# A two-layer graph attention kernel: the order of aggregation, projection and transposition in steps 3 to 5 of layer 0

## The reference, cut to what matters

```python
# layer 0 (adj holds only 0 and 1, so only a0 takes part)
e     = leaky(einsum('bid,bjd->bij', x * a0, x))        # leaky slope 0.2
alpha = sigmoid(where(adj == 1, e, -max))
x1    = layernorm(x + einsum('bij,bjd->bid', alpha, x) + bias)
# layer 1
Hh = x1 @ W;  s = Hh @ a_src;  d = Hh @ a_dst
e  = where(adj != 0, exp(-leaky_relu(s[:, :, None] + d[:, None, :], 0.2)), 0)
h  = elu((e @ Hh) / rowsum(e))
out = layernorm(x1 + h)
```

## Time and profile before

| | us |
|---|---|
| median of 3 runs | 1378.3 (1376.89 to 1379.58) |
| profiled execution, its own time | 1379.31 |
| span of the profiled execution | 1377.5 |
| PE busy | 1277.8 (93%) |
| DVE busy | 1030.4 (75%) |
| ACT busy | 855.3 (62%) |
| POOL busy | 841.3 (61%) |

### The profile page before, as it was taken

How to read it: one execution, slowest core, us unless ns; L and a number is a source line. 1 busy time by engine, 2 the same in 40 slices (tenths; PEclk the granted TensorE clock), 3 DMA queues, 4 the chain that set the end, 5 groups by cost and what they waited for, 6 DMA issues and landing times.

```text
span 1377.5 us, 27394 instructions
## 1 busy us (share of the span) xinstructions
PE 1277.8 (93%) x7874; PEld 1142.0 (83%) x7874; DVE 1030.4 (75%) x2594; ACT 855.3 (62%) x2129; POOL 841.3 (61%) x1228
## 2 busy tenths in 40 slices
PE   3899999999999999999999999999999998999986
PEld 3788888888888888988888888888888888888875
DVE  3677878777787777778777787877778777787864
ACT  3665757567574765757567574765757567574642
POOL 4465838557394765838567394765838567394732
PEclk9999999999999999999999999999999999999998
DMA  6344251623406143251623406143250623406001
GB/s 142 61 77 101 40 103 47 110 72 63 109 11 126 57 82 97 42 105 40 110 72 65 107 16 121 57 86 93 45 109 32 110 72 65 107 15 122 27 5 33
DMA packets 190352, 101.73 MB, mean 74 GB/s; under 512 B 140656, under 2 KB 173808, under 8 KB 190320
## 3 DMA queue, kind: packets, MB, share of 16 engines
q1 hardware_dynamic: 171888, 67.79, 20.9%
q0 software_dynamic: 18432, 33.56, 14.5%
HBM read 84.55 MB, written 16.78 MB: 74 GB/s over the span
## 4 chain that ended last, share of the span: by engine, by line
PE 39%; POOL 24%; DVE 19%; issue 11%; ACT 5%; DMA 1%; DVEq 0%; POOLq 0%; SPq 0%; ACTq 0%
POOL coef_lo L368 13%; PE acc_bank L1207 11%; PE hh_bank L1186 5%; DVE coef L867 5%; PE acc_bank L1088 4%; PE acc_bank L1090 4%; PE acc_bank L1089 4%; PE lg_bank L1088 3%; PE lg_bank L1090 3%; PE lg_bank L1089 3%; POOL var_eps L376 3%; POOL rstd L379 2%; POOL rstd L389 2%; DVE stats L907 2%; DVE reluP L902 2%
## 5 line engine op out<-in xcount | busy, mean ns | idle before, releaser
L1207 PE MATMUL acc_bank<-H,coef 128*128 128x258 f32 x2048 | 468.9, 383 | 10.4 <-ACT reluP L607 9.1
L1207 PEld LDWEIGHTS acc_bank<-H,coef 128*128 128x128 f32 x2048 | 382.7, 190 | 72.1 <-issue 18.1
L368 POOL TENSOR_TENSOR coef_lo<-coef,coef_hi 128x1024 fp32r<-128x1024 f32 x128 | 306.0, 2392 | 77.4 <-ACT coef_hi L553 75.6
L1088 PE MATMUL acc_bank<-h_hi,coef_hi 128*128 128x256 f32 x1024 | 297.9, 291 | 1.8 <-issue 1.8
L1090 PE MATMUL acc_bank<-h_hi,coef_lo 128*128 128x256 f32 x1024 | 286.9, 280 | 0.0
L1089 PE MATMUL acc_bank<-h_lo,coef_hi 128*128 128x256 f32 x1024 | 286.8, 280 | 0.0
L867 DVE SCALAR_TENSOR_TENSOR coef<-tr_bank,E_col,codeT 128x256 f32<-128x256 f32 x512 | 209.1, 476 | 39.3 <-PE acc_bank L1207 36.8
L1088 PEld LDWEIGHTS acc_bank<-h_hi,coef_hi 128*128 128x128 f32 x1024 | 195.2, 191 | 2.9 <-issue 2.0
L1089 PEld LDWEIGHTS acc_bank<-h_lo,coef_hi 128*128 128x128 f32 x1024 | 195.8, 191 | 0.0
L1090 PEld LDWEIGHTS acc_bank<-h_hi,coef_lo 128*128 128x128 f32 x1024 | 195.5, 191 | 0.0
L553 ACT ACTIVATE coef_hi<-coef 128x1024 fp32r<-128x1024 f32 x128 | 135.6, 1060 | 86.5 <-DVE coef L806 86.1
(11 more groups left out here) (76 smaller groups left out, 2280.3 us busy)
## 6 DMA issues: line engine op xcount, KB each, us to landing
code_nat<-in_adj POOLq DMA_DIRECT2D x128, 256.0 KB, 5.0
x_raw<-in_x SPq DMA_DIRECT2D x16, 1024.0 KB, 5.6
out<-x SPq DMA_DIRECT2D x128, 128.0 KB, 1.7
codeT<-code_nat SPq DMA_TRANSPOSE x128, 3.3
W_ext<-in_L_gnn_W SPq DMA_DIRECT2D x1, 256.0 KB, 2.8
score<-in_L_gnn_a SPq DMA_DIRECT2D x1, 256.0 KB, 6.8
bias_bc<-in_L_gnn_bias SPq DMA_DIRECT2D x1, 128.0 KB, 3.5
a_col<-in_L_gnn_a SPq DMA_DIRECT2D x4, 1.0 KB, 2.1
```

The costliest lines, as they stand in the source:

```text
L368: nc.gpsimd.tensor_tensor(coef_lo[:, t % 4, :, :], blocks(coef[:, t % 4, :]), f32(coef_hi[:, t % 4, :, :]), ALU.subtract).then_inc(S.lo0, 1)
L1088: nc.tensor.matmul(dst, lhs_hi, rhs_hi, start=first, stop=False)
L1207: ins = nc.tensor.matmul(acc_bank[t % 2][:, 0:HC], coef[:, SLOT1[t], J * P:(J + 1) * P], H[:, J, :], start=J == 0, stop=J == NT - 1)
```

## The change

In PE's list, steps 3 to 6 now run the aggregation of `t` first, then `project(t-3)`, then `T(t-2)`. Step 2 loses `project(0)`, which goes to step 3; step 6 gets a second projection, `project(4)`, at its end, so that from step 7 on the order is the old one. The transpositions of columns (`spread_G`) of tiles 0 to 2 move from step 5 to step 6.

In ACT's list, `keep_H(t-3)` and `keep_x1T(t-2)` of steps 3 to 6 move from the head of the step to behind `high0` and `watch_codes`; in steps 3 to 5 `watch_codes` moves behind `high0`. In step 5 the pair now stands ahead of `norm1` of the graph before.

In DVE's list, `low_xT` stands ahead of `norm0` in steps 2 to 5, as it did before only in step 5.

```diff
 # ACT
                 for t in range(NT + 1):
-                    if t >= 3:
+                    if t >= 7:
                         keep_H(F, b, t - 3, prev, False)
-                    if t >= 2:
+                    if t == 2 or t >= 7:
                         keep_x1T(F, b, t - 2, prev)
                     if nxt and t in XT_STEP:
                         high_xT(F, b + 1, XT_STEP[t], False)
-                    if t < 6:
+                    if t < 3:
                         watch_codes(b, t)
                     if 1 <= t and t + 3 < NT:
                         high0(F, b, t + 3, prev)
+                    if 3 <= t < 6:
+                        watch_codes(b, t)
+                    if 3 <= t < 7:
+                        keep_H(F, b, t - 3, prev, False)
+                        keep_x1T(F, b, t - 2, prev)
                     if t == 5 and prev:
                         norm1(F, b - 1, NT - 1)
 # DVE
-                    if nxt and t == 5:
+                    if nxt and t in XT_STEP:
                         low_xT(F, b + 1, XT_STEP[t], False)
                     if t >= 1:
                         norm0(F, b, t - 1, prev)
-                    if nxt and t < 5 and t in XT_STEP:
-                        low_xT(F, b + 1, XT_STEP[t], False)
 # PE
                 for t in range(NT):
-                    if t >= 3:
-
-                        pe.wait_ge(F.x1T_kept, NT * b + t - 2)
-                        transpose_x1(F, b, t - 2)
+                    if t == 7:
+                        pe.wait_ge(F.x1T_kept, NT * b + 5)
+                        transpose_x1(F, b, 5)
                     if 1 <= t and t + 3 < NT:
                         mirror(b, t + 3)
                     aggregate0(F, b, t, prev)
-                    if t == 2:
-                        if prev:
-
-                            pe.wait_ge(F.x1T_kept, NT * b)
-                        transpose_x1(F, b, 0)
-                    if t >= 3:
-                        project(F, b, t - 2, prev)
-                    if t == 5:
+                    if 3 <= t < 7:
+                        project(F, b, t - 3, prev)
+                    if 2 <= t < 7:
+                        if t >= 3 or prev:
+
+                            pe.wait_ge(F.x1T_kept, NT * b + t - 2)
+                        transpose_x1(F, b, t - 2)
+                    if t == 6:
                         for u in range(3):
                             spread_G(b, u)
-                    if t >= 6:
-                        spread_G(b, t - 3)
+                    if t == 7:
+                        project(F, b, 5, prev)
+                        spread_G(b, 4)
...
-                    if t == 2:
-                        project(F, b, 0, prev)
+                    if t == 6:
+                        spread_G(b, 3)
+                        project(F, b, 4, prev)
```

## The result

The changed kernel takes 1396.65 us (median of 4 runs, 1394.63 to 1400.07), the kernel before beside it 1378.94 (1376.89 to 1380.97): a ratio of 1.0131, 95% interval 1.0104 to 1.0158. It is 18 us slower; 1394 was forecast. The profiled execution took 1400.07 us by its own time, its span is 1398.4 and the mean granted clock 0.979 (before 0.990). They differ a little in the kernels of the experiments too; the names of the tiles say which instruction a row is.

A forecast was written before the change was run, and what follows sets the result against it. PE, busy 93% of the span, was taken as the bound. New waits of 4.47 us against 3.58 lost, with a slower stretch +0.96 a graph, gave 15.4 us over 16 graphs: some 1394 us for the median, range 1379 to 1404.

The forecast's parts named there:

- the four losses go: PE's waits ahead of `project(0)`, `T(1)`, `T(2)` and `T(3)`, 3.58 us a graph in all, vanish in PE's new order.
- the copies are what is late: ACT's copy of `T(1)`, queued behind `high0` and `watch_codes`, makes PE's `project(1)` wait 2.68 us a graph.
- the mask of tile 6 can't end sooner: On DVE: ready a microsecond sooner, it still ends at 318.41, held by POOL's `low0` of tile 5.
- the normalisation loses to `low0`: In step 3 DVE's normalisation of tile 2 waits out POOL's `low0` of tile 6: `x1` at about 322.14.
- The lead that I gave as 0.15 us: POOL's `low0` of tile 6 starts 0.15 us ahead of DVE's normalisation of tile 2 in step 3.
- the second wait: PE's `project(2)` waits 1.79 us a graph for ACT's copy of `T(2)`, behind a later mask of tile 7.
- two a graph and some 65: Sign in the profile after: `project` waits for ACT twice a graph, near 2.5 and 1.7 us, some 65 us in all.
- +0.96 a graph: Sum on PE: new waits of 4.47 us against 3.58 lost now, +0.89, and one more slower aggregation.
- The term of 0.07: On PE: aggregation 3, behind a wait, ran 0.07 us slower than aggregation 4; one more such stretch was added.
- the third rival: Lateness lasts past step 5: with POOL 1 us later, `T(5)` waits 0.7 more, about 1405 us; chance 0.12.
- first rival: PE no longer waits, as `low0` does not hold the mask: -1.6 a graph, about 1353 us; chance 0.11.
- second: The normalisation wins the race in step 3 or need not wait: +0.2 a graph, 1381 to 1382 us; chance 0.15.

The follow-up runs named there:

- Kernel 6: The changed kernel with `watch_codes` of steps 3 to 5 behind `keep_H` and the copy instead of ahead of them: 1391.06 us, ratio 1.0106.
- kernel 2: The changed kernel with ACT's order undone, `keep_H` and the copy at the head of each step again: 1403.3 us, ratio 1.0219.
- Kernels 1: The changed kernel with DVE's order undone, `low_xT` behind `norm0` in steps 2 to 4: 1385.07 us, ratio 1.0056.
- 5: The changed kernel with POOL waiting for `norm0` of steps 3 and 4 before `low0` of tiles 6 and 7: 1389.74 us, ratio 1.0092.
- 10: The kernel before with DVE's edit alone, `low_xT` ahead of `norm0` in steps 2 to 4: 1400.24 us, ratio 1.0169.
- Kernel 3: The changed kernel with DVE's and ACT's orders both undone, leaving PE's order alone: 1357.03 us, ratio 0.9856.
- kernel 9: The changed kernel with DVE's order undone and `watch_codes` of steps 3 to 5 behind `keep_H` and the copy: 1362.05 us, ratio 0.989.

## Why the prediction was right, step by step

- **Held: the four losses go, and the copies are what is late.** The copy of `T(1)` ended 20.11 us into the graph, predicted 20.08; PE's wait, from start to start 323.94 - (320.89 + 0.12), is 2.93 (2.68 predicted), as PE was there 0.2 us sooner than reckoned. Kernel 6 takes the wait down by 1.13, to 1.64, by taking `watch_codes` out of its way, and in kernel 2, with ACT's old order, it is gone.
- **Held: the mask of tile 6 can't end sooner.** 16.93 against 16.96, though it began 0.9 us earlier. No run took this hold away, but the traces of all kernels bear it out: in the second to fifteenth graph the mask of tile 6 begins anywhere from 14.68 to 15.69 us into the graph, and always ends 1.01 or 1.02 behind `low0` of tile 5.
- **Held: the normalisation loses to `low0`.** 2.43 and 2.48 us; `x1` of tile 2 at 20.68 (20.69 predicted), mask of tile 7 at 23.06 (23.05). The lead that I gave as 0.15 us was 0.07, and 0.05 in step 4 (0.05 to 0.14 over all graphs): the race was closer than I said, and POOL won it in all fifteen graphs that have it. Kernels 1, 5 and 10 show the cost by taking the hold away or adding it alone. The Trainium skill ("SBUF — State Buffer", section "SBUF: two separate sides") gives this as an exclusive lock of the pair of ports for a whole instruction; the rows agree, with 2.43 and 2.35 us where POOL began first and 0.40 where DVE did.
- **Held in sum, its parts shifted: the second wait.** In the fifth graph it is 413.73 - (411.94 + 0.12) = 1.67 from start to start (1.79 predicted; 1.50 in the bracket), the two waits together 4.60 against 4.47. In the graphs with a stretch at half clock, half of them, that stretch takes its place and costs nothing more; so the list has 25 waits and 54.8 us where I had two a graph and some 65.
- **Size a little off: +0.96 a graph** was 1.15. The waits give 4.60 - 3.58 = 1.02 of it. The term of 0.07 for a slower aggregation "behind a wait" had the wrong reason: in the kernel after aggregations 3 and 4 take 2.91 (313.74 to 316.65, 318.10 to 321.01) with no wait ahead of them, and why is open. The rest of the difference to 1394 is the fourteenth graph (the third rival, once) and the clock in the third and the last graph.
- **Luck: the clock.** That it could fall stood in no term. It came out nearly free only because the second wait was behind it; kernel 2, which has no such wait, lost some 14 us of its profiled execution to it.
- **The rivals.** PE's waits did not vanish (first rival). Kernel 3 shows that 1.5 us of them are left, and 81.25 us a graph against 82.48 (824.81 / 10) before, once ACT's copies are at the head and DVE's order is the old one. `low0` did not lose the race (second), and POOL's lateness reached `T(5)` in one graph of sixteen (third).

## What to carry to other kernels

When an engine's order is changed, ask of every engine that is "ordered to match" what stands ahead of the one instruction the bottleneck waits for: a queue that is worked in order and waits for a mask carries that wait to everything behind it. Undo parts one at a time and together: here two delays each hid the other, so single edits gave 12 and 6 us and both 35. And look whether an instruction is moved to where another engine's long operation begins: a start 0.07 us ahead of it or 0.05 us behind it decided over 2 us.

## What the runs showed of the hardware

- DVE's normalisation, begun 0.05 to 0.14 us behind POOL's subtraction of 2.4 us, ended 0.15 us behind it in every case: 0.40 us became 2.35 to 2.50. Begun 0.07 us ahead it took 0.40 (kernel 2). The mask, which reads two SBUF tensors, was held likewise. `low_xT`, which has one of its inputs in a bank, was not; it ran beside `low0` of tile 6 (319.58 to 321.99) in the kernel before, no slower than with POOL free of `low0` (0.69 at 327.11):

```profile
319.58 0.68 DVE L753 TENSOR_TENSOR hT_lo<-lg_bank,hT_hi 128x512 fp32r<-128x512 f32 x1
```

- PE's clock fell to 1.2 GHz behind waits of 2.4 to 2.8 us in some graphs and not in others with the same waits. It also fell behind 1.56 us in two of the fourth to thirteenth graph of the kernel before, and behind 1.64 and 0.65 us in four of them in kernel 6; in kernel 9 (1.3 to 1.5 us) it fell in none. With a later wait the stretch was free (83.57 and 83.66 us), without one it cost 1.4 us (83.95 against 82.52). 20 extra transposes in the wait kept the clock up in the fourth to thirteenth graph. The Trainium skill, page "TensorE: Matmul & The Clock Gate", section "HAM oscillation — how this bites in real kernels", also has idle gaps between products as what throttles the clock again; the rows agree in so far as every such stretch of a middle graph stands behind a wait. That it depends here on more than the length of the wait is left open.
- POOL stood 2.27 to 2.42 us between two DMA issues in the fourteenth graph of every kernel, the one before too; the cause is open.
